# Cross-attention, 16 head groups in a row: context splits and layer-norm pieces given to other steps of the heads' pipeline

## The reference

```python
def _cross_attention(q_in, kv_in, wq, bq, wk, bk, wv, bv, wo, bo, bias_k, bias_v):
    qh = (q_in @ wq + bq).reshape(b, q_len, H, K)
    kh = (kv_in @ wk + bk).reshape(b, t, H, K)
    vh = (kv_in @ wv + bv).reshape(b, t, H, K)
    ...
    weights = jax.nn.softmax(jnp.einsum("bqhk,bthk->bhqt", qh, kh) / scale, axis=-1)
    return jnp.einsum("bhqt,bthk->bqhk", weights, vh).reshape(b, q_len, H * K) @ wo + bo
...
h = _layer_norm(x, ln1_scale, ln1_offset)
x = x + _cross_attention(h, xf_1, ...)
h = _layer_norm(x, ln2_scale, ln2_offset)
x = x + _cross_attention(h, xf_2, ...)
```

## Time and profile before

| | |
|---|---|
| median of 3 runs | 2338.5 us (2337.21 to 2339.63) |
| profiled execution, its own time | 2342.8 us |
| its span, first to last instruction | 2341.0 us |
| PE busy | 2223.7 us (95%) |
| DVE / ACT / POOL busy | 1608.0 (69%) / 1175.2 (50%) / 932.8 us (40%) |
| share of PE in the chain that ended last | 76% (DVE 12%, ACT 5%) |
| stretch of the heads' pipeline | about 30 to 1650 us |
| mean granted clock of PE | 0.976 |

### The profile page before, as it was taken

One profiled execution on the slowest core, in us unless ns is written; L12 is line 12 of the kernel. 1 busy time (PEld: TensorE's weight loads), 2 busy tenths in 40 slices (PEclk: granted clock), 3 DMA queues, 4 the chain that ended last, 5 costly groups with the idle time before them and its releaser, 6 DMA issues.

```text
span 2341.0 us, 37135 instructions
## 1 busy us (share of the span) xinstructions
PE 2223.7 (95%) x12724; PEld 2162.0 (92%) x12724; DVE 1608.0 (69%) x3636; ACT 1175.2 (50%) x2834; POOL 932.8 (40%) x903
## 2 busy tenths in 40 slices
PE   7999999999998999999899999989999899988899
PEld 6999999999998999999899999989989788877899
DVE  5767677777777777677777778776574685567443
ACT  4555455554545555454555555455233565466232
POOL 4314344242343414243341434421899132212487
PEclk8999999999999999999999999999999999999899
DMA  3646445554644546455454645544434212111243
GB/s 132 137 82 147 97 109 98 118 125 81 150 101 101 107 107 124 104 129 107 101 121 86 147 99 114 130 79 67 153 108 116 77 50 72 46 38 28 57 124 112
DMA packets 137494, 238.69 MB, mean 102 GB/s; under 512 B 32992, under 2 KB 75104, under 8 KB 137312
## 3 DMA queue, kind: packets, MB, share of 16 engines
q1 hardware_dynamic: 137312, 236.32, 45.0%
HBM read 214.96 MB, written 4.92 MB: 94 GB/s over the span
## 4 chain that ended last, share of the span: by engine, by line
PE 76%; DVE 12%; ACT 5%; issue 4%; DMA 2%; POOL 1%; SPq 0%; DVEq 0%; POOLq 0%; ACTq 0%
PE bank L760 72%; PE bank L846 2%; DVE U L1409 2%; PE bank L1033 1%; DVE ctxN L1413 1%; ACT U L1160 1%; DVE lnb L1456 1%; DVE ln_c L1463 1%; DVE tmp L1525 1%; DVE kT L1409 1%; DVE hT L1409 1%; DVE pT L1413 1%; DMA ctxN_raw<-in_ctx 1%; DVE prob L1579 1%; DVE prob L1492 1%
## 5 line engine op out<-in xcount | busy, mean ns | idle before, releaser
L680 POOL TENSOR_SCALAR mring<-stage 128x512 fp32r<-128x512 f32 x325 | 228.6, 703 | 1074.0 <-PE bank L760 932.2
L760 PE MATMUL bank<-ctxT,kring 128*128 128x362 f32 x3456 | 628.7, 329 | 0.0
L760 PEld LDWEIGHTS bank<-ctxT,kring 128*128 128x128 f32 x3456 | 582.8, 189 | 3.0
L760 PE MATMUL bank<-pT,ctxN 128*128 128x400 f32 (+1 forms) x2304 | 474.5, 354 | 8.8 <-DVE U L1413 8.8
L682 POOL TENSOR_TENSOR mring<-stage,mring 128x512 fp32r<-128x512 f32 x325 | 436.3, 1343 | 27.1
L760 PEld LDWEIGHTS bank<-pT,ctxN 128*128 128x128 f32 (+1 forms) x2304 | 419.0, 192 | 10.4 <-issue 10.3
L760 PE MATMUL bank<-hT,mring 128*128 128x400 f32 x1608 | 322.7, 350 | 8.5 <-DVE hT L1409 6.4
L760 PE MATMUL bank<-U,mring 128*128 128x400 f32 x1536 | 312.3, 357 | 2.9 <-POOL mring L682 2.9
L760 PEld LDWEIGHTS bank<-hT,mring 128*128 128x128 f32 x1608 | 298.9, 191 | 11.7 <-issue 9.8
L760 PEld LDWEIGHTS bank<-U,mring 128*128 128x128 f32 x1536 | 282.1, 193 | 3.8 <-POOL mring L682 3.5
L1413 DVE TENSOR_TENSOR U<-bank,U 128x400 fp32r<-128x400 f32 x256 | 145.8, 571 | 172.6 <-ACT U L1160 172.6
(11 more groups left out here) (102 smaller groups left out, 3005.0 us busy)
## 6 DMA issues: line engine op xcount, KB each, us to landing
ctxT_raw<-in_ctx SPq DMA_DIRECT2D x72, 724.0 KB, 7.4
ctxN_raw<-in_ctx SPq DMA_DIRECT2D x256, 192.0 KB, 3.0
stage<-in_wk SPq DMA_DIRECT2D x64, 256.0 KB, 4.6
stage<-in_wq SPq DMA_DIRECT2D x64, 256.0 KB, 2.7
stage<-in_wv SPq DMA_DIRECT2D x64, 256.0 KB, 3.8
stage<-in_wo SPq DMA_DIRECT2D x64, 256.0 KB, 2.7
stage<-in_fa SPq DMA_DIRECT2D x64, 256.0 KB, 2.6
stage<-in_fb SPq DMA_DIRECT2D x64, 256.0 KB, 2.6
```

Of the source, the lines that this page charges most:

```text
L680: nc.gpsimd.tensor_scalar(hi, src, 1.0, 1.0, ALU.mult, ALU.mult).then_inc(S.w_hi, 1)
L760: mm = pe.matmul(dst, parts_l[a], parts_r[b], start=first and k == 0, stop=last and k == len(order) - 1)
```

## The change

No computation is added or removed; the numbers of instructions and SP's and POOL's orders stay the same, word for word. In the diff POOL's due times come first, then PE, then ACT, then DVE. What moves are rows on ACT and DVE, and one row on PE per norm group:

- The split of the sequence with i % 4 == 1 (keys of u = 4 to 7) moves from u = 1 (ACT) and u = 1, 2 (DVE) to u = 3, ahead of the tails. That of i % 4 == 2 (keys of u = 8 to 11) keeps its place on ACT (u = 5); its two DVE halves move from the ends of u = 5 and 6 to u = 7, ahead of the tails.
- The four ctxN splits that all stood in u = 4 go to u = 4, 5, 7 and 8.
- Norm groups: centring from u = 1, 2 to u = 3, squares from u = 1, 2 to the end of u = 3, variance product, square root and scale from u = 3 to u = 6, reciprocals from u = 4, 5 to u = 8, 9, the last high parts from u = 7, 8 to u = 11, 12, the last low parts from u = 8, 9 to u = 11, 12 and 13, where the last two stand ahead of the tails.
- PE's waits follow: the value product of u = 4 waits for the centring instead of the square root, the projection of u = 7 waits for the square root, the variance product waits for the value addition.

```diff
+VAR_STEP = 6
+def natural_split_step(un):
+    return natural_load_step(un) + ({0: 0, 1: 1, 2: 3, 3: 4}.get(un % 16, 0) if un >= DC else 0)
...
+CONTEXT_HIGH, CONTEXT_LOW = {}, {}
+for i_ in range(2, 4 * GN):
+    CONTEXT_HIGH[4 * (i_ - 1) + [3, 1, 1, 1][(i_ - 1) % 4]] = i_
+    for k_ in range(2):
+        CONTEXT_LOW.setdefault(4 * (i_ - 1) + [3, 3, 1 + k_, 1 + k_][(i_ - 1) % 4], []).append((i_, k_))
...
-                extra += [(n0 - 6.5, 0, norm_sum, li), (n0 + 2.5, 0, norm_square_sum, li), (n0 + 6.5, 0, norm_scale, li)]
+                extra += [(n0 - 6.5, 0, norm_sum, li), (n0 + 3.6, 0, norm_square_sum, li), (n0 + 9.4, 0, norm_scale, li)]
...
             def norm_var(li):
                 pe.wait_ge(S.ln_ss, 3 * li)
+                if li <= 4:
+                    pe.wait_ge(S.v_tmp, HG * HG * li - HG)
...
                     if G % HG == 2:
-                        pe.wait_ge(S.ln_std, G // HG + 2)
+                        pe.wait_ge(S.ln_cent, DC * (G // HG + 2))
...
                         if h == 0:
                             pe.wait_ge(S.v_tmp, HG * G + HG)
+                            if G % HG == 2:
+                                pe.wait_ge(S.ln_std, G // HG + 2)
...
-                if norm_at(n, 3):
-                    norm_var(norm_at(n, 3))
+                if norm_at(n, VAR_STEP):
+                    norm_var(norm_at(n, VAR_STEP))
...
+                if n in CONTEXT_HIGH and n % 4 == 3:
+                    context_high(CONTEXT_HIGH[n])
...
-                if n % 4 == 1 and n // 4 + 1 in range(2, 4 * GN):
-                    context_high(n // 4 + 1)
+                if n in CONTEXT_HIGH and n % 4 != 3:
+                    context_high(CONTEXT_HIGH[n])
...
                 if norm_at(n, 3):
-                    norm_std(norm_at(n, 3))
-                    norm_scale(norm_at(n, 3))
+                    norm_square(norm_at(n, 3))
+                if norm_at(n, VAR_STEP):
+                    norm_std(norm_at(n, VAR_STEP))
+                    norm_scale(norm_at(n, VAR_STEP))
+                if norm_at(n, 11):
+                    norm_high(norm_at(n, 11), (0, 1))
+                if norm_at(n, 12):
+                    norm_high(norm_at(n, 12), (2, 3))
...
+                for i, k in CONTEXT_LOW.get(n, ()):
+                    if n % 4 == 3:
+                        context_low(i, k)
+                if norm_at(n, 13):
+                    norm_low(norm_at(n, 13), (2, 3))
                 for kind, G, k in tails(n):
                     if kind == "u":
                         value_sum_low(G, k)
+                        if norm_at(n, 3) and k in (13, 14):
+                            norm_centre(norm_at(n, 3), (2 * (k - 13), 2 * (k - 13) + 1))
...
+                if norm_at(n, 8):
+                    norm_rstd(norm_at(n, 8), (0,))
+                if norm_at(n, 9):
+                    norm_rstd(norm_at(n, 9), (1,))
+                if norm_at(n, 11):
+                    norm_low(norm_at(n, 11), (0,))
+                if norm_at(n, 12):
+                    norm_low(norm_at(n, 12), (1,))
```

More of the change, by code:

```diff
@@ L1314, in _ @@
                     context_high(1)
-                for un in NATURAL.get(n, ()):
+                for un in SPLIT_NATURAL.get(n, ()):
                     if un % 16 == 15:
                         natural_high(un)
+                if n in CONTEXT_HIGH and n % 4 == 3:
+                    context_high(CONTEXT_HIGH[n])
                 for kind, G, k in tails(n):
@@ L1324, in _ @@
                         query_high(G, k)
-                for un in NATURAL.get(n, ()):
+                for un in SPLIT_NATURAL.get(n, ()):
                     if un % 16 != 15:
                         natural_high(un)
-                if n % 4 == 1 and n // 4 + 1 in range(2, 4 * GN):
-                    context_high(n // 4 + 1)
[L1330 to L1333, removed]
-                if norm_at(n, 3):
-                    norm_std(norm_at(n, 3))
-                    norm_scale(norm_at(n, 3))
[L1337 to L1340, removed]
+                if n in CONTEXT_HIGH and n % 4 != 3:
+                    context_high(CONTEXT_HIGH[n])
+                if norm_at(n, 3):
+                    norm_square(norm_at(n, 3))
[6 more added lines that the diff above has]
+                    norm_high(norm_at(n, 12), (2, 3))
             def mlp_steps(m):
@@ L1677, in _ @@
                         query_low(G, k)
-                for un in NATURAL.get(n, ()):
+                for un in SPLIT_NATURAL.get(n, ()):
                     if un % 16 != 15:
                         natural_low(un)
[L1681 to L1690, removed]
+                for i, k in CONTEXT_LOW.get(n, ()):
+                    if n % 4 != 3:
+                        context_low(i, k)
                 if norm_at(n, 8):
-                    norm_low(norm_at(n, 8), (0, 1))
+                    norm_rstd(norm_at(n, 8), (0,))
                 if norm_at(n, 9):
-                    norm_low(norm_at(n, 9), (2, 3))
+                    norm_rstd(norm_at(n, 9), (1,))
[3 more added lines that the diff above has]
+                    norm_low(norm_at(n, 12), (1,))
             def mlp_steps(m):
```

3 lines of the change are left out of this document (2 added, 1 removed).

## The result

The changed kernel takes 2351.45 us (median of 5 runs, 2351.01 to 2352.95), the kernel before 2338.51 us (5 runs, 2337.21 to 2342.85). The ratio is 1.0058, with a 95% interval of 1.0047 to 1.0069: slower by 0.6%, and beyond the 0.2% that a measurement here can tell. The forecast was 2351.5 us.

What follows compares the result with a forecast made beforehand. PE works 95% of the span, so only its waits and the slow stretches behind them count. +22.5 - 14.7 - 2.5 - 11.6 - 6.8 + 26.1 = +13.0 us on 2342.8 gives 2355.8, or 2351.5 on the median; own range 2340 to 2361.

Steps and rivals of the forecast that it cites:

- The U wait of step 3: Step 3, 15 groups: PE's third value sum starts 1.5 us late behind the ctxT halves, 22.5 us lost.
- rival 2: Step 3 does not wait either, as the sums' low parts keep ahead of PE: -35 us, 2303; chance 0.04.
- The query's wait: Step 13, groups 3, 7, 11: next query waits 6.0 us for normed input, plus 2.7 us clock, 26.1 us lost.
- Rival 1: Step 13: the query waits only 0 to 2 us, total 2325 to 2331, faster; chance 0.19.
- Rival 3: POOL's later scaling pushes the ctxN load back, up to 3.4 us in step 13 of three groups: 2362; chance 0.14.
- Rival 4: The clock also falls after step 3's 1.5 us waits, 15 by up to 1.5 us: 2374; chance 0.08.
- The norm groups' steps 6 to 8: Four norm groups: waits for square root and ctxT replace the kT wait, 5.0 instead of 6.7 us, 6.8 won.
- the sum without the drain: Steps 6 to 8: table loads counted without the skill page's 1.38 us drain each; with it, the sum would be 2362.5.
- The old wait of the norm groups in step 3: Step 3, four norm groups: the 2.01 us wait and the slow sums behind it go, 14.7 us back.
- The groups with G % 4 = 2: Step 6, four groups: kT wait falls from 2.38 to 1.0 us and the clock stays up, 11.6 us won.
- the kT of the seven other groups: Step 6, groups with G % 4 = 0 or 1: the 0.36 us kT wait goes, 2.5 us won.
- The 4.3 us taken off at the end: Whole kernel: the profiled execution's 2342.8 us stood 4.3 us above the runs' median, so the sum was lowered by that.

Runs made afterwards that it cites:

- Run 2: Changed kernel with the ctxT splits of step 3 put back in steps 1 and 2, as in the kernel before: 2330.07 us.
- Run 1: Changed kernel with the norm's last high parts at the end of step 11, last low parts in steps 11 and 12 ahead of the tails: 2325.19 us.
- run 4: Changed kernel with the norm's high parts at the end of step 11, low parts 2 and 3 at the head of DVE's step 13: 2345.34 us.
- run 3: Changed kernel with both edits: norm's last pieces in steps 11 and 12, and step 3's ctxT splits back in steps 1 and 2: 2300.35 us.
- run 9: Changed kernel with earlier norm pieces, step 3's ctxT back, step 7's low halves in step 6, POOL's norm sum after step 7's logits: 2282.03 us.
- run 5: Kernel before with only three of four ctxN splits spread over steps 5, 7 and 8, and step 8's ctxT low halves in step 7: 2309.14 us.
- run 7: Kernel before with the norm's moves alone, all splits as before: 2328.89 us.
- run 6: Kernel before with only the ctxT of step 4 split in step 3, ahead of the value sums: 2363.4 us.

## Why the prediction held, point by point

- **The U wait of step 3** was read rightly: right place, right count, 1.35 us of idle time against 1.5. Its price was 1.61 us, not the idle time. The waits of 0.36 us that went are the same: 0.55 us each came back. Where PE had not waited at all, the stall costs 0.2 to 0.26 us beyond what the timeline shows as idle. Run 2 shows that the ctxT halves are the whole cause. With this wait rival 2 is out.
- **The query's wait** was read rightly in place, cause and total, 5.22, 6.11 and 6.75 us against 6.0 each, but not term by term. In group 7 the two ACT high parts (799.70 to 800.83) ran beside DVE, so the 1.0 us put on them cost nothing; normalise, whose own length the sum left out, took 0.41 us; and the load came later for PE, with ACT's split 1.11 us behind the time at which PE wanted the query (799.27 against 804.27 - 6.11 = 798.16) where the earlier trace rows had 0.30 us (801.08 against 800.78). That these errors cancel is luck. The slow clock behind it cost about 2 us each (4.34 against 2.36 us for the query), not 2.7, which had been read behind another wait. Run 1 shows the cause, run 4 its two parts. Rival 1 needed the load in time; ACT waited 4.96 us for it in group 7, and 4.00 before.
- **Rival 3** is out: if POOL's scaling had pushed the load back, ACT would wait longer for it in the norm groups. It waits 3.89, 4.96 and 5.15 us in groups 3, 7 and 11, and 3.73 to 5.28 us in the eleven other groups from 1 to 14. The push itself was there: SP issues this load 1.33 us behind the transposes of step 12 in the three groups, against 0.5 us or less in the others and 0.6 us or less in the trace of before. But ACT's split of it begins 6.51, 7.58 and 7.77 us behind these transposes, in the others 6.35 to 7.89 us, so it lands no later, as the rival's "against" had it.
- **Rival 4** is out: behind all 15 waits of 1.35 us the 18 products took 3.53 or 3.54 us, at a granted clock of 1.00 in the stretch shown above.
- **The norm groups' steps 6 to 8** were worth 4.5 us in all, not 6.8. The mechanism was right (the root first, then the normalise behind two table loads, then ctxT). The waits were a little shorter than their terms, 0.53 us for the root against 1.0 and 2.29 us for ctxT against 2.5. The clock stays low from the keys to the projection (2.97, 1.11, 0.70 and 2.67 us; in run 3, where it was kept, 2.23, 0.66, 0.42 and 2.45 us) and cost the 1.5 us taken: the three steps take 21.46 us in group 7 and 19.94 us there in run 3. What the sum left out is the variance product, which moves here from step 3: the stretch of step 6 takes 3.45 us with it and without a wait (752.64 to 756.09), against 2.76 us in groups without it, 0.69 us each and 2.8 us in all. The Trainium skill (page "ScalarE: Activation LUTs", section "What ACT_TABLE_LOAD costs") would put some 1.4 us of drain behind each load; the rows above have the root 1.29 us behind the first load's start and the exponent 1.30 us behind the second's, so the trace does not agree and the sum without the drain was the right one.
- **The old wait of the norm groups in step 3** gave back 17.9 us, not 14.7, but the same variance product leaves step 3, so some 2.8 us of the 17.9 are not won, only moved. With it booked in one place the two rows of the norm groups come to -15.1 and -7.3 us, close to the forecast's -14.7 and -6.8.
- **The groups with G % 4 = 2** were mis-sized, 8.9 us against 11.6: a reading of one row for four. Behind the 2.38 us wait of group 6 the twelve products took 3.98 us; in the same trace they took 3.68, 2.44 and 2.45 us in groups 2, 10 and 14. So only 3.1 us of clock could come back, where 6.0 had been counted. The wait itself fell to 0.91 us, against 1.0, and run 9 shows that POOL's additions were the rest of it.
- **Not foreseen:** a wait of 1.12 us for ctxT in step 8 of group 0, in place of one of 0.44 us for kT two steps later; the low halves in step 7 stand too late there, too.
- The parts don't add, and the prediction had this right where it counted: splits alone take 16.7 us from steps 6 to 8 of the norm groups, the norm's move alone 18.4, both 4.5. Each removes the same wait, and together they make a new one.

The errors are of both signs: +1.7 us on U and +2.7 us on the kT of the groups with G % 4 = 2, and -1.4 us each on the kT of the seven other groups and on the query. That the median came out within 0.1 us of the forecast is luck at that level; over the pipeline the forecast was 1.6 us off (13.0 against 14.6). The 4.3 us taken off at the end were right in kind: the profiled execution of before lost 3.8 us ahead of the pipeline, which is no property of the kernel: in the trace of run 1, where nothing differs so early, the first transposes come as late (50.5 us, against 50.2 before and 46.3 in the changed kernel).

## What to carry to other kernels

When an operation is moved out of a busy step, count the queue of the step that receives it just as exactly: here three moves each made something late that PE wanted at once (a sum's low part, a query's input, the next keys), and each moved piece could stand in a step where nobody waited for it. Put what is wanted soon ahead of an operation that waits for a load, not behind. Try each part alone and undo each part: two of the three parts of this change were gains by themselves (runs 5 and 7), and the third, with two bad placements in the others, turned what could be 2.3% faster into 0.6% slower.

## What the runs showed of the hardware

**The same wait may cost clock or not.** Behind the kT wait of 2.38 us (kernel before, runs 6 and 7: 12 cases) the twelve products took 3.68 to 3.98 us in six cases and 2.43 to 2.45 us in the other six. Behind the ctxT wait of 2.26 to 2.30 us (changed kernel, runs 1 to 4: 20 cases) the keys were slow in 14 and not in six. In run 3 both kinds stand in one trace:

```profile
351.32 2.80 PE L773 MATMUL bank<-ctxT,kring 128*128 128x362 f32 x12 [2.29 <-DVE ctxT L1428]
...
745.74 2.23 PE L773 MATMUL bank<-ctxT,kring 128*128 128x362 f32 x12 [2.29 <-DVE ctxT L1428]
```

Between the first transposes and the last no wait of 1.93 us or less was followed by slow products in these traces, and each of 3.89 us or more was. What decides between the two at 2.0 to 2.4 us is open. A price for the waits between should be taken as a mean over cases, with the spread kept for the range.
